# Mamba layer and 16 experts on one core: the gates' products move ahead of the first expert, and GpSimd waits for the scatters before it ends

## The reference, cut to what matters

```python
x = L0_attn_x                                  # (8, 512, 128)
x = x + _L0_attn_ref(_layernorm(x), ...)       # a Mamba layer, a scan over 512 steps
x = x + _L0_ffn_ref(_layernorm(x), Wg, w1, w2) # 16 experts

def _L0_ffn_ref(x, Wg, w1, w2):                # xr: the 4096 tokens as rows
    C = (S + E - 1) // E                       # 256 places for each expert
    gate = softmax(xr @ Wg); idx = argmax(gate, axis=1)
    ...                                        # loc: the token's place in its expert
    dispatched = zeros((E, C + 1, d)).at[idx, min(loc, C)].set(xr)[:, :C]
    h = relu(einsum('ecm,emf->ecf', dispatched, w1))
    expert_out = einsum('ecf,efm->ecm', h, w2)
    return expert_out[idx, min(loc, C - 1)] * (gates_s * valid)[:, None]
```

## Time and profile before

| | |
|---|---|
| median of 3 runs | 697.07 us (696.28 to 697.87) |
| the profiled execution's own time | 697.41 us |
| its span (first to last instruction) | 695.6 us |
| PE, DVE, ACT, POOL busy | 88%, 80%, 75%, 83% of the span |
| HBM read, written | 69.61 MB, 11.72 MB |
| mean granted clock of TensorE | 0.962 of full |

### The profile page before, as it was taken

How to read it: one execution, slowest core, us unless ns; L and a number is a source line. 1 busy time by engine, 2 the same in 40 slices (tenths; PEclk the granted TensorE clock), 3 DMA queues, 4 the chain that set the end, 5 groups by cost and what they waited for, 6 DMA issues and landing times.

```text
span 695.6 us, 12853 instructions
## 1 busy us (share of the span) xinstructions
PE 613.1 (88%) x4108; PEld 476.9 (69%) x4108; DVE 556.2 (80%) x891; ACT 520.0 (75%) x1011; POOL 580.6 (83%) x411
## 2 busy tenths in 40 slices
PE   8689999999899999989999998999989893699774
PEld 6237676767668677767767776777867782589673
DVE  5558899999999999999999999999988985613221
ACT  3699989999999999999999999999968612112120
POOL 5178999999999999999999999998889961267775
PEclk9889999999999999999999999999999997599997
DMA  4251533236145423714442362334135205346541
GB/s 101 82 150 63 168 100 129 64 116 206 59 149 158 126 72 98 217 68 149 131 142 57 111 194 95 119 95 155 58 109 173 79 2 126 100 128 205 183 145 32
DMA packets 59977, 81.95 MB, mean 118 GB/s; under 512 B 14829, under 2 KB 40722, under 8 KB 59910
## 3 DMA queue, kind: packets, MB, share of 16 engines
q1 hardware_dynamic: 56400, 74.79, 34.4%
q0 software_dynamic: 2560, 6.08, 2.9%
q10 hardware_dynamic: 950, 0.27, 0.2%
HBM read 69.61 MB, written 11.72 MB: 117 GB/s over the span
## 4 chain that ended last, share of the span: by engine, by line
POOL 60%; issue 22%; PE 9%; DVE 4%; DMA 3%; POOLq 1%; ACTq 0%; SPq 0%; ACT 0%; DVEq 0%
POOL h L837 29%; POOL h L851 19%; POOL u L824 3%; PE ps L588 3%; PE ps L575 2%; POOL fac L866 1%; DMA z<-rows_d,gidx 1%; POOL out_dram L398 1%; POOL z L390 1%; POOL lnp L798 1%; POOL rstd L873 1%; PE ps L1636 1%; PE ps L555 1%; POOL cq L861 1%; DMA b0b<-b_d 1%
## 5 line engine op out<-in xcount | busy, mean ns | idle before, releaser
L1360 DVE TENSOR_TENSOR_SCAN h<-ps,h 128x902 f32<-128x902 f32 x204 | 319.9, 1609 | 20.8 <-ACT ps L977 12.0
L837 POOL TENSOR_TENSOR h<-u,scr 128x1280 f32<-128x1280 f32 x104 | 283.5, 2742 | 2.4
L1752 PEld LDWEIGHTS ps<-h,ident 128*128 128x128 f32 x1632 | 224.6, 190 | 21.8 <-issue 17.3
L1752 PE MATMUL ps<-h,ident 128*128 128x160 f32 x1632 | 231.0, 300 | 1.1 <-issue 0.8
L1086 ACT ACTIVATE z<-dtb,asc 128x240 f32<-128x240 f32 (+3 forms) x432 | 201.5, 536 | 0.1
L977 ACT ACTIVATE ps<-z 128x820 f32<-128x820 f32 (+1 forms) x208 | 138.0, 688 | 22.6 <-DVE h L1360 18.9
L851 POOL TENSOR_TENSOR h<-h,scr 128x1280 f32<-128x1280 f32 (+1 forms) x52 | 138.0, 2654 | 0.6 <-DVE h L1376 0.6
L1411 DVE TENSOR_TENSOR h<-h,ps 128x640 f32<-128x640 f32 (+1 forms) x155 | 87.9, 578 | 0.5 <-issue 0.2
L1636 PE MATMUL ps<-xnT,wT 128*128 128x488 f32 x144 | 70.8, 602 | 0.0
L987 ACT ACTIVATE sqb<-h 128x208 f32<-128x208 f32 x102 | 44.9, 442 | 26.2 <-DVE h L1360 23.5
L390 POOL DMA_INDIRECT z<-rows_d,gidx x32 | 33.3, 1041 | 34.8 <-DVE gidx L496 25.4
(11 more groups left out here) (201 smaller groups left out, 810.6 us busy)
## 6 DMA issues: line engine op xcount, KB each, us to landing
scr<-b_d SPq DMA_DIRECT2D x52, 640.0 KB, 4.8
scr<-c_d SPq DMA_DIRECT2D x52, 320.0 KB, 4.4
z<-in_L_ffn_w_dram SPq DMA_DIRECT2D x32, 256.0 KB, 3.2
xx_d<-xx SPq DMA_DIRECT2D x8, 256.0 KB, 2.0
xxr<-xx_d SPq DMA_DIRECT2D x8, 256.0 KB, 2.6
rows_d<-h2b SPq DMA_DIRECT2D x16, 120.0 KB, 2.1
rows_d<-xxr SPq DMA_DIRECT2D x16, 120.0 KB, 2.2
out_dram<-xxr SPq DMA_DIRECT2D x16, 120.0 KB, 2.5
```

The source lines that it names most:

```text
L837: pool.tensor_tensor(hr[:, hf * RH:(hf + 1) * RH, 1:SLOT].rearrange("p (n b) t -> p n b t", b=B), us.unsqueeze(1).to_broadcast([P, NST, B, ...
L1360: dve.tensor_tensor_scan(hs, region(G)[:, 0:(r1 - r0) * SLOT], hs, 0.0, ALU.mult, ALU.add).then_inc(gscan, 1)
L1752: pe.matmul(ps[:, YB, 0:H * BS], ident[:], hr[:, :, n * B:(n + 1) * B, 0:SEG], start=(n == 0), stop=False)
```

## The change

Three edits. On PE `gates()` goes from behind `turn(1)` to ahead of `turn(0)`. On DVE the sum of the gates' parts (`gs`) goes ahead of `relu(0, 0)`. POOL gets one more wait behind its last scatter, for all 32 scatters' landing.

```diff
@@ pool_tail
                 scatter(e)
                 if e + AHEAD < E:
                     gather(e + AHEAD)
+            pool.wait_ge(scattered, 16 * NS)
@@ dve_tail
-            relu(0, 0)
             dve.wait_ge(gates_done, 1)
             dve.tensor_reduce(gs, ps[:, GATES, 0:3 * NS].rearrange("p (f c) -> p c f", c=NS), AX_X,
                               ALU.add).then_inc(gs_ready, 1)
             dve.wait_ge(gs_ready, 1)
+            relu(0, 0)
             take_out(0)
             relu(1, 1)
@@ pe_tail
             for _ in range(16):
                 pe.matmul(ps[:, PRE, 0:P], ident[:], ident[:], start=True, stop=True)
+            gates()
             turn(0, 0)
             up(0, 0)
             turn(1, 1)
-            gates()
             pe.wait_ge(idx_ready, 2)
             down(0, 0)
             up(1, 1)
```

## The result

| | before | changed |
|---|---|---|
| median of 6 runs each, one chip | 696.67 us (695.95 to 697.87) | 699.88 us (699.17 to 702.12) |
| ratio | | 1.0047 [1.0028, 1.0065] |
| the profiled execution's own time, its span | 697.41, 695.6 | 702.12, 700.3 |

Its profiled execution is the slowest of its six; the three quickest took 699.17 to 699.53. So its trace shows the mechanism, but more of it than the median holds.

The account below looks back on a forecast made before the run. POOL's pace from first scatter to last, then its drain, was taken to bound the kernel. +0.5 (start) and +1.25 (drain) on the profiled 697.41 gave 699.2, stated as 698.9 against the median; range 697.0 to 701.3.

Parts of the forecast that it names:

- What bounds the kernel: POOL's own pace from first scatter to last, 52 instructions in 68.86 us; a later first scatter moves the end equally.
- The move at full clock: Start of the experts on PE: gates' products from 607.2, `down(0)` ending at 618.6 against 619.58, a gain of 1.0 us.
- Rival 3: PE's clock does not fall, or falls where it costs little: +0.25 us, 697.3; chance 0.12.
- The clock: PE's clock is low for 3.4 us from 612.5, slowing `up(0)`: +0.5 us for the first scatter and the end.
- rival 1: PE's clock stays low for longer, `up(0)` and `down(0)` slow: start +2.4 to +3.0, time 700.7 to 701.3; chance 0.22.
- the 623: Sign of being wrong: POOL's first scatter past 623 (clock low for long), where 621.5 to 622.0 was expected.
- POOL waiting for DVE at more than its first two scatters: Named among the signs that the prediction would be wrong, in the changed kernel's profile; no size given.
- Rival 4: At POOL's end, the drain's work runs beside the wait, which then costs nothing: +0.5 us, 697.6; chance 0.10.
- The drain: POOL's last drain starts 1.25 us later behind the wait and still costs 5.3 us, 83 ns per indirect DMA: +1.25.
- rival 2: POOL's final drain only waits and has no work of its own: -3.5 us, 693.6; chance 0.13.
- rival 5: POOL's final drain takes its 8.04 us whenever it starts: +4.0 + 0.5, 701.6; chance 0.07.
- Sum by parts: Whole kernel: +0.5 for the start and +1.25 for the drain, +1.75 us in all.

Follow-up runs that it names:

- e3_drain_mid: The kernel before with one more drain in POOL's program, behind its first 12 gathers; 696.65 us against 697.10, ratio 0.9990 [0.9975, 1.0004].
- e1_move_only: The changed kernel without POOL's added wait (gates' move and DVE's order only); 698.48 us against 697.10 for the kernel before, ratio 1.0020.
- e8_after_second_look: The changed kernel itself, run again on the slower chip; 712.67 us (one run), kernel before 707.30 there.
- e2_wait_only: The kernel before with only POOL's wait for all scatters added; 698.65 us against 697.10, ratio 1.0017 [1.0006, 1.0028].
- e9_after_third_look: The changed kernel itself, run once more on the slower chip; 713.78 us (one run), kernel before 707.30 there.
- e10_halved_with_wait: The kernel before with the gates' products in two halves around `up(0)`, plus POOL's wait, on the slower chip; 709.62 us against 707.30, ratio 1.0025.
- e6_gates_halved: The kernel before with the gates' 32 products in two halves around `up(0)`, no POOL wait; 694.89 us against 697.53, ratio 0.9964.

## Why the prediction was right, and where it was off

The measured time, 699.88 us, lies in the range and on the predicted side; the change costs 3.2 us where 1.75 was the sum. The time itself came nearer (698.9 said) in part by luck, as the kernel before had its median at 697.07 over the three runs that were known and at 696.67 over six.

**What bounds the kernel: right on the chips where the kernel before takes 697.** In the changed kernel a later first scatter moved the end by the same amount. The 52 POOL instructions behind it took 68.92 us (69 predicted), and 68.3 to 69.2 in every kernel with all its scatters on those chips; at the low end is e3_drain_mid, whose body gave back 0.6 of a first scatter 1.0 late. On the chip where it takes 707 the body is 77.5 to 81.3, and POOL's pace is not what bounds it.

**The move at full clock: right in place.** The gates' products started at 607.5 (607.2 predicted), the two gaps were 0.55 and 1.16 us (0.55 and 1.1), and `gs` cost nothing. The start's agreement is luck: that execution was 1.3 us late by then, and behind its first gather the start lay at 3.4 us where 4.4 was forecast; e1_move_only has the 4.3. Rival 3, full clock all along, was seen in no profile of the changed order.

**The clock: right in kind, too small in size.** It fell within 0.2 us of the gates' end or up to 1.5 us ahead of it in the profiles of the changed order (612.3 against 613.07 in the changed kernel, 611.1 against 612.62 in e8_after_second_look, 611.9 against 611.66 in e1_move_only). The term that was mis-sized is "Let the low stretch begin at 612.5 and last 3.4 us again": it lasted 3.4 us in e1_move_only, and there the lead grew by 0.53 as forecast (+0.5). It lasted 6.8 in e8_after_second_look, with `down(0)` still at full clock, and 10.2 in the two others, which is rival 1 with its slow `down(0)`. By time the move costs 1.4 us [0.4, 2.4], not 0.5. The forecast took the likeliest case for the typical one, though rival 1 had 0.22; 1.4 lies between the two cases. The profiled execution was rival 1's: its first scatter, at 624.5, or 623.2 without that execution's late start, is past the 623 that the prediction had named as a sign of being wrong, and `up(0)` took 3.75 us where 2.5 to 3.6 was said. Its lead grew by 1.96 (+2.4 to +3.0 predicted for rival 1); the gates' start 1.0 us earlier than forecast, behind the first gather, is what took it below.

Another sign, POOL waiting for DVE at more than its first two scatters, could tell nothing: POOL waited at six in the kernel before and at six in the changed one. And the chances are added up wrongly: 0.36, 0.22 and 0.07 make at most 0.65 for slower, not 0.66, and rivals 3 and 4 alone 0.22 for within, not 0.21. That moves nothing here.

The Trainium skill (TensorE: Matmul & The Clock Gate, Part 1, What's actually happening) says that the throttled state is the default and that activity releases it. The rows agree in the main: the clock came back after 3.4 us at a dense f32 stretch in the earlier trace rows, and 10.2 us were seen only where the same work lay in pieces between gaps. But it stayed low for 6.8 us in e2_wait_only without a gap, and for 3.4 in e1_move_only with both, so the gaps alone do not set it; how late it comes back differs between executions of one program.

**The drain: right, as near as it can be told.** The term was +1.25, from 5.3 us behind the landing. Its work's start moved from the last scatter's end to 0.2 us behind the landing that SP sees, 1.4 us in all, and it took 5.294. The estimate of 83 ns for each indirect DMA measured 82. That refutes rival 2 (693.6, the drain only waits) and rival 5 (8.04 us whenever it starts). Rival 4, its work beside the wait, would need e2_wait_only at no cost; it costs 1.2 us [0.4, 2.0], and its trace has the whole 5.294 us behind the wait. The rule of the Trainium skill weighed there (PSUM — Partial Sum Buffer, Engine vs sequencer instructions) holds as far as it goes, but POOL's drain has work of its own in these runs.

**Sum by parts.** Forecast 0.5 + 1.25 = 1.75. Measured by parts 1.4 + 1.2 = 2.6, and for the whole 3.2 [2.0, 4.5]. The missing 0.6 is inside the intervals; no run shows a cost of the two together beyond their sum.

## What to carry to other kernels

Look at what every wait stands in front of: a wait ahead of an engine's last drain is not free when the drain has work of its own that would have run beside the landing. Moving thin products out from under a stall does not get rid of the stall, it uncovers the latencies that they lay over; splitting them, half over each gap, covered both and here kept the clock up. It paid 2.5 us on one chip, and nothing that could be measured on a chip where another delay bounded the experts. And where the granted clock falls inside the stretch that an edit touches, one profile is one draw: take the mean over several, or time one part at a time.

## What the runs showed of the hardware

- GpSimd's drain works off its indirect DMAs at 82 ns each: 5.294 us for 64, 3.987 for 48, 4.31 for 52, the first of them the same to the nanosecond in all six profiles with the wait. An earlier drain takes its share off the last. Each of these DMAs moved 128 rows.
- With the same number of the gates' products at the same pace, the clock fell when all 32 stood in one row (PE busy without a pause; nine profiles of nine) and stayed at 1.00 when they stood as 16 and 16 around f32 products of 256 columns (four of four), or when an f32 product followed every third (the one profile).
- The low clock costs these bf16 products of 96 columns nothing: 5.53 us for the 32 in e1_move_only, all at full clock, and 5.53 in e2_wait_only with the last 2.7 us at 0.50. The f32 products behind them took up to 1.9 times as long at it (`up(0)` 3.75 against 1.96, `down(0)` 3.75 in e9_after_third_look against 1.96).
- Chips differ by 10 us in the time of the kernel before, 697 against 707 to 708. The trace places it in the experts: the body is 77.5 to 81.3 us there and 68.3 to 69.2 on the others. In e10_halved_with_wait DVE starts the gates' sum 2.4 us and `take_out(0)` 3.6 us after PE's last recorded product, where in e6_gates_halved the sum starts 0.04 us after it. What is late was not tried; that PE idles 2.03 us ahead of `up(1)` there says that it is more than late records.
